# A transformer half-block's first normalisation taken inside its local attention's block

## What is computed

```
x = x + 0.5 * ffn(layernorm(x))      # first pass
x = x + attention(layernorm(x))      # 16 heads, with a line memory
x = x + 0.5 * ffn(layernorm(x))      # second pass, the same weights
```

```
h = shift_token(x)                   # the upper 64 channels come from the token before
q, k, v = split(h @ wqkv)            # 8 heads of 64
q = l2norm(q) * q_scale; k = l2norm(k) * k_scale
q, k = rotary_xpos(q, k)
o = local_attention(q, k, v)         # windows of 64: own window and the one before
x = x + o @ wo
h = layernorm(shift_token(x)) * ln_g + ln_b
a, g = split(h @ w1 + b1)
x = x + (a * gelu(g)) @ w2 + b2
```

## Time and profile before

| | us |
|---|---|
| median of three runs | 2052.03 (2050.5 to 2053.05) |
| profiled execution, its own time | 2047.57 |
| its span, first to last instruction | 2045.7 |
| PE busy | 1932.3 (94%), mean granted clock 0.974 |
| DVE busy | 1623.9 (79%) |
| ACT busy | 1502.1 (73%) |
| POOL busy | 911.3 (45%) |

### The profile page before, as it was taken

The page is one execution under the profiler, slowest core; times in us unless marked ns, Lnnn a source line. Parts: engine busy times, 40 slices in busy tenths (PEclk is TensorE's granted clock), DMA queues, the critical chain, the costliest instruction groups (busy, mean ns, idle before and its releaser), DMA issues. The chain is left out here.

```text
span 2045.7 us, 53721 instructions
## 1 busy us (share of the span) xinstructions
PE 1932.3 (94%) x19002; PEld 1163.5 (57%) x19002; DVE 1623.9 (79%) x5186; ACT 1502.1 (73%) x4129; POOL 911.3 (45%) x538
## 2 busy tenths in 40 slices
PE   6999999999999979999999978778999999999998
PEld 3677774577774334444444357426777745777753
DVE  5899974899994378999999459748999748999944
ACT  4899993699996353777777844348999946999962
POOL 1778860578870150000000046107788604888800
PEclk9999999999999986999999999899999999999999
DMA  5121220112220040111111000002122201122201
GB/s 173 42 45 43 47 65 5 34 42 46 47 67 12 0 145 30 42 43 43 43 42 41 9 3 2 1 6 46 42 47 47 65 6 33 41 47 47 63 16 42
DMA packets 75966, 84.88 MB, mean 41 GB/s; under 512 B 17124, under 2 KB 50484, under 8 KB 75572
## 3 DMA queue, kind: packets, MB, share of 16 engines
q1 hardware_dynamic: 75407, 81.41, 16.1%
q10 hardware_dynamic: 292, 0.03, 0.0%
HBM read 20.88 MB, written 8.39 MB: 14 GB/s over the span
## 5 line engine op out<-in xcount | busy, mean ns | idle before, releaser
L303 ACT ACTIVATE probs<-probs,negmax 128x128 f32<-128x128 f32 x1024 | 399.9, 396 | 25.7 <-DVE negmax L376 23.7
L1438 DVE TENSOR_REDUCE maxes<-ps_global 128x1 f32<-128x512 f32 (+3 forms) x640 | 362.2, 629 | 24.8 <-PE ps_global L1342 18.5
L1507 ACT ACTIVATE gprobs<-ps_global 128x1024 f32<-128x1024 f32 (+3 forms) x384 | 290.7, 811 | 124.1 <-PE ps_global L1379 101.8
L258 POOL TENSOR_TENSOR rot<-rot 128x1024 f32<-128x1024 f32 x128 | 302.2, 2361 | 130.1 <-DVE rot L346 130.1
L264 POOL TENSOR_TENSOR qk<-rot,cnorm 128x1024 f32<-128x1024 f32 x128 | 243.7, 1904 | 119.4 <-POOL rot L258 88.1
L271 POOL TENSOR_TENSOR probs<-probs,iden 128x1024 f32<-128x1024 f32 x128 | 242.7, 1896 | 119.1 <-DVE iden L384 119.1
L376 DVE CUSTOM_DVE_ANT_0 probs<-ps_attn,masks 128x128 f32<-128x128 f32 x1024 | 225.9, 284 | 0.0
L1337 PE MATMUL ps_global<-ks,qs 48*128 48x512 bf16 (+3 forms) x768 | 196.8, 347 | 11.4 <-DMA ks<-split_scratch 9.6
L303 ACT ACTIVATION_READ_ACCUMULATOR probs<-probs,negmax 128x1 f32 x1024 | 196.9, 192 | 0.0
L344 DVE TENSOR_TENSOR rot<-ps_attn,rotary 128x512 f32<-128x512 f32 x256 | 174.8, 683 | 11.2 <-PE ps_attn L170 8.5
L238 PEld LDWEIGHTS ps_attn<-probsT,v_first 128*64 128x64 f32 x2048 | 118.1, 136 | 98.1 <-ACT probsT L324 93.6
(11 more groups left out here) (203 smaller groups left out, 4574.7 us busy)
## 6 DMA issues: line engine op xcount, KB each, us to landing
v_first<-v_second SPq DMA_DIRECT2D x256, 128.0 KB, 2.3
hs<-z_a SPq DMA_DIRECT2D x256, 32.0 KB, 1.9
ln<-z_b SPq DMA_DIRECT2D x56, 128.0 KB, 2.3
split_scratch<-parts SPq DMA_DIRECT2D x8, 384.0 KB, 3.3
split_scratch<-gprobs SPq DMA_DIRECT2D x8, 384.0 KB, 4.7
qs<-split_scratch SPq DMA_DIRECT2D x32, 96.0 KB
ks<-split_scratch SPq DMA_DIRECT2D x32, 96.0 KB
x_tok<-in_x_dram SPq DMA_DIRECT2D x4, 512.0 KB, 6.5
```

Source lines behind the costliest of these rows:

```text
L258: nc.gpsimd.tensor_tensor(a, a, b, ALU.add).then_inc(C["rot_sum"], 1)
L303: last = nc.scalar.activation(probs[:, k % 2, slot, :], probs[:, k % 2, slot, :], ACT.Exp, scale=-1.0, bias=negmax[:, k % 2, slot:slot + 1 ...
L1438: nc.vector.reduce_max(maxes[:, n % 2, r, p0:p1, t, c], ps[:, bank_of(use), 0:len(both) * w].rearrange("q (p s) -> q p s", s=w), AX_X).the ...
L1507: nc.scalar.activation(probs[:, step % RING, 2 * p:2 * p + 2, 0:w], ps[:, S0 + 2 * p:S0 + 2 * p + 2, 0:w], ACT.Exp).then_inc(C["p2_exp"], 1)
```

## The change

The normalisation that opens a pass no longer has a block: it becomes "layer -1" of `local_attention_pass`, its six stages the functions that the layers' inner normalisations use already (`pe_centre`, `pe_var`, `act_ln_square` and so on), with three pairs of PSUM banks of its own (`FIRST_PAIRS`). The calls `body(0, -4)` to `body(0, -1)` are replaced, in both passes, by orders written out for each engine, in which chunks and the stages of tiles 0 to 3 alternate. A shift of tile 0, 4, 8 ... waits for its chunk's scale. `FirstUse`, given in the first pass only, replaces `RotaryTables` and `Folds`: `wqkv` is loaded from setup's queue, the other 14 loads behind the shifts of tiles 0 to 3; the masks' cast and seven products come ahead of scale 0 on DVE and the eighth behind it; the fold's matmuls and additions close the fill; POOL's scaling of `w1` and its cast move to the end of layer 0, ahead of `gp_ln_low`. The tables, rows and masks are loaded into the memory of `probs` and `probsT`. The normalisation ahead of the middle part stays a block.

```diff
+FIRST_PAIRS = ((3, 4), (5, 6), (7, 2))
+
+
+def local_attention_pass(nc, C, K, W, probs, probsT, z_in, z_out, x, first):
...
-            if i >= B and k % 4 == 0:
+            if k % 4 == 0 and i >= B:
                 mlp_wait1(sp, "mlp_out", 0, (BATCH_TILES * (i - B) + k) // 4)
+            elif k % 4 == 0:
+                ln_wait(sp, "ln_out", -1, (BATCH_TILES * i + k) // 4)
...
+        def ln_banks(layer, m):
+            return FIRST_PAIRS[m % 3] if layer < 0 else LN_PAIRS[m]
...
-            centred, var = LN_PAIRS[m]
-            if m == CHUNKS - 1:
+            centred, var = ln_banks(layer, m)
+            if layer < 0:
+                if m >= 3:
+                    ln_wait(pe, "ln_out", layer, m - 3)
+            elif m == CHUNKS - 1:
...
-            nc.tensor.matmul(ps[:, centred, :], K["centre"][:, :], ln_h[:, m % 4, :], start=True, stop=True
-                             ).then_inc(C["ln_centred"], 1)
+            nc.tensor.matmul(ps[:, centred, :], K["centre"][:, :], x[:, columns(m)] if layer < 0 else ln_h[:, m % 4, :],
+                             start=True, stop=True).then_inc(C["ln_centred"], 1)
...
-                if folds is not None and (i, k) == (0, -3):
-                    folds.tensor(pe, ps[:, OB, :])
...
+            pe_centre(pe, wait, -1, 0)
+            pe_centre(pe, wait, -1, 1)
+            pe_var(pe, wait, -1, 0)
+            pe_centre(pe, wait, -1, 2)
+            pe_var(pe, wait, -1, 1)
+            pe_centre(pe, wait, -1, 3)
+            pe_var(pe, wait, -1, 2)
+            pe_var(pe, wait, -1, 3)
+            pe_centre(pe, wait, -1, 4)
+            if first is not None:
+                first.tensor_projections(pe)
+            pe_project_keys(pe, wait, *t(0, 0))
+            pe_project_queries(pe, wait, *t(0, 0))
+            pe_centre(pe, wait, -1, 5)
+            pe_var(pe, wait, -1, 4)
+            pe_centre(pe, wait, -1, 6)
+            pe_var(pe, wait, -1, 5)
+            pe_project_keys(pe, wait, *t(0, 1))
+            pe_project_queries(pe, wait, *t(0, 1))
+            pe_centre(pe, wait, -1, 7)
+            pe_var(pe, wait, -1, 6)
+            pe_var(pe, wait, -1, 7)
+            pe_project_values(pe, wait, *t(0, 0))
+            wait_shifted(pe, *t(0, 2))
+            pe_project_queries(pe, wait, *t(0, 2))
+            pe_project_keys(pe, wait, *t(0, 2))
+            ln_wait(pe, "ln_out", -1, 7)
+            pe_transpose_qk(pe, wait, *t(0, 0))
+            pe_project_values(pe, wait, *t(0, 1))
+            pe_await_scores(pe, wait, *t(0, 0))
+            pe_scores(pe, *t(0, 0))
+            pe_transpose_qk(pe, wait, *t(0, 1))
+            pe_project_keys(pe, wait, *t(0, 3))
+            pe_project_queries(pe, wait, *t(0, 3))
+            pe_project_values(pe, wait, *t(0, 2))
+            pe_await_scores(pe, wait, *t(0, 1))
+            pe_scores(pe, *t(0, 1))
+            if first is not None:
+                first.tensor(pe, ps[:, OB, :])
+            pe_transpose_qk(pe, wait, *t(0, 2))
...
+                if first is not None and layer == 0:
+                    first.gpsimd(gp)
                 gp_ln_low(gp, wait, layer)
...
+            gp_rotary_sum(gp, wait, *t(0, 0))
+            gp_rotary_scale(gp, wait, *t(0, 0))
+            gp_rotary_sum(gp, wait, *t(0, 1))
+            gp_rotary_scale(gp, wait, *t(0, 1))
+            gp_rotary_sum(gp, wait, *t(0, 2))
+            gp_rotary_scale(gp, wait, *t(0, 2))
+            gp_normalise(gp, wait, *t(0, 0))
+            gp_rotary_sum(gp, wait, *t(0, 3))
...
+            act_ln_square(act, -1, 0)
+            act_ln_square(act, -1, 1)
+            act_ln_log(act, -1, 0)
+            act_ln_inverse(act, -1, 0)
+            act_ln_square(act, -1, 2)
+            act_ln_log(act, -1, 1)
+            act_ln_inverse(act, -1, 1)
+            act_ln_square(act, -1, 3)
+            act_ln_log(act, -1, 2)
+            act_ln_inverse(act, -1, 2)
+            act_ln_log(act, -1, 3)
+            act_ln_square(act, -1, 4)
+            act_ln_inverse(act, -1, 3)
+            act_square_q(act, wait, *t(0, 0))
+            act_square_k(act, wait, *t(0, 0))
+            act_ln_square(act, -1, 5)
+            act_ln_log(act, -1, 4)
+            act_ln_inverse(act, -1, 4)
+            act_ln_square(act, -1, 6)
+            act_ln_log(act, -1, 5)
+            act_norm(act, wait, *t(0, 0))
+            act_ln_inverse(act, -1, 5)
+            act_square_q(act, wait, *t(0, 1))
+            act_ln_square(act, -1, 7)
+            act_square_k(act, wait, *t(0, 1))
+            act_ln_log(act, -1, 6)
+            act_ln_log(act, -1, 7)
+            act_ln_inverse(act, -1, 6)
+            act_ln_inverse(act, -1, 7)
+            act_norm(act, wait, *t(0, 1))
+            act_values(act, wait, *t(0, 0))
+            act_square_q(act, wait, *t(0, 2))
+            act_qT(act, wait, *t(0, 0))
+            act_kT(act, wait, *t(0, 0))
+            act_square_k(act, wait, *t(0, 2))
+            act_values(act, wait, *t(0, 1))
+            act_qT(act, wait, *t(0, 1))
+            act_kT(act, wait, *t(0, 1))
+            act_norm(act, wait, *t(0, 2))
+            act_exp(act, wait, *t(0, 0), range(0, 3))
+            act_square_q(act, wait, *t(0, 3))
+            act_exp(act, wait, *t(0, 0), range(3, 8))
+            act_square_k(act, wait, *t(0, 3))
+            act_qT(act, wait, *t(0, 2))
+            act_exp(act, wait, *t(0, 1), range(0, 2))
...
+            if first is not None:
+                first.vector_tables(dve, range(0, 7))
+            dve_ln_scale(dve, -1, 0)
+            if first is not None:
+                first.vector_tables(dve, range(7, 8))
+            dve_ln_scale(dve, -1, 1)
+            dve_ln_scale(dve, -1, 2)
+            dve_rotate(dve, wait, 1, *t(0, 0))
+            dve_ln_scale(dve, -1, 3)
+            dve_rotate(dve, wait, 0, *t(0, 0))
+            dve_ssq(dve, wait, *t(0, 0))
+            dve_ln_scale(dve, -1, 4)
+            dve_rotate(dve, wait, 1, *t(0, 1))
+            dve_clip_norm(dve, wait, *t(0, 0))
+            dve_ln_scale(dve, -1, 5)
+            dve_rotate(dve, wait, 0, *t(0, 1))
+            dve_ssq(dve, wait, *t(0, 1))
+            dve_ln_scale(dve, -1, 6)
+            dve_ln_scale(dve, -1, 7)
+            dve_clip_norm(dve, wait, *t(0, 1))
+            dve_rotate(dve, wait, 1, *t(0, 2))
+            dve_rotate(dve, wait, 0, *t(0, 2))
+            dve_ssq(dve, wait, *t(0, 2))
+            dve_max(dve, wait, *t(0, 0))
+            dve_clip_norm(dve, wait, *t(0, 2))
+            dve_rotate(dve, wait, 1, *t(0, 3))
+            dve_rotate(dve, wait, 0, *t(0, 3))
+            dve_inv(dve, wait, *t(0, 0))
+            dve_max(dve, wait, *t(0, 1))
+            if first is not None:
+                first.vector(dve, ps[:, OB, :])
...
                 sp_shift(sp, wait, *t(0, tile))
+            if first is not None:
+                first.sync_loads(sp)
             sp.wait_ge(C["pass_set"], C.after("pass_set", 2))
...
+            sp.dma_start(W["wqkv"][:, :, :], dram["wqkv"].rearrange("l p n -> p l n")).then_inc(C["wqkv_in"], 16)
...
+class FirstUse:
...
     def sync_loads(self, sp):
         C, A, W, dram = self.C, self.A, self.W, self.dram
-        sp.dma_start(W["wqkv"][:, :, :], dram["wqkv"].rearrange("l p n -> p l n")).then_inc(C["wqkv_in"], 16)
-        sp.dma_start(W["wo"][:, :, :, :], dram["wo"].rearrange("l (c p) n -> p l c n", p=128)).then_inc(C["wo_in"], 16)
         sp.dma_start(W["w1"][:, :, :], dram["w1"].rearrange("l p n -> p l n")).then_inc(C["w1_in"], 16)
         for j, (f0, m) in enumerate(HID_BLOCKS):
             sp.dma_start(W["w2"][0:m, :, j, :], dram["w2"][:, f0:f0 + m, :].rearrange("l p n -> p l n")).then_inc(C["w2_in"], 16)
+        sp.dma_start(W["wo"][:, :, :, :], dram["wo"].rearrange("l (c p) n -> p l c n", p=128)).then_inc(C["wo_in"], 16)
         for name in ATTENTION_LOADS:
             dst = A[name]
             sp.dma_start(dst[tuple(slice(None) for _ in dst.shape)], dram[ATTENTION_LOADS[name]]).then_inc(C["as_in"], 16)
 
-    def tensor_last(self, pe):
+    def tensor_projections(self, pe):
         C = self.C
         pe.wait_ge(C["wqkv_in"], C.after("wqkv_in", 16))
-        pe.wait_ge(C["wo_in"], C.after("wo_in", 16))
...
+    def vector_tables(self, dve, products):
+        nc, C, K, W = self.nc, self.C, self.K, self.W
+        for m in products:
+            if m == 0:
+                dve.wait_ge(C["mask_in"], C.after("mask_in", 16))
+                nc.vector.tensor_copy(K["masks"][:, :, :], W["masks_f"])
+                dve.wait_ge(C["rotary_in"], C.after("rotary_in", 16 * N_ROWS))
+            layer, which = m // 4, m % 4
+            nc.vector.tensor_tensor(W["rotary"][:, layer, :, which, :], W["tables"][:, :, which, :],
+                                    W["rows"][:, layer, which, :].unsqueeze(1).to_broadcast([P, T // TILE, DH]), ALU.mult)
...
+        with ExitStack() as first:
+            probs, probsT = attention_probs(first)
```

(11 more changed lines are left out.)

92 lines of the change are left out of this document (23 added, 69 removed).

## The result

The changed kernel took **2017.94 us** (median of 4 runs, 2015.32 to 2019.93), the kernel before 2051.66 on the same chip; ratio **0.9835**, interval 0.9818 to 0.9852. That is 33.7 us faster, where 25.8 were forecast.

The account below looks back on a forecast made before the run. The two fills, 54.22 and 50.57 us with no engine full, were taken as what the change could shorten; gains of 13.9 and 11.9, together 25.8, off the runs' median 2052.0 gave 2026.2 us, range 2018 to 2037.

Parts of the forecast that it names:

- the yardstick: DVE's first copy of turned probabilities of tile 0: whatever brings it forward brings the layer's end forward by as much.
- the two fills: Stretches from each pass's normalisation block to DVE's first copy: 54.22 and 50.57 us, forecast to become 40.3 and 38.7.
- rival 1: Loose weave in the fills: late hops put scale 7 and the transposes 6 us later; gain 14, 2038; chance 0.20.
- Rival 2: Weave in the fills tighter than placed: 2014 to 2019 us; chance 0.05.
- Rival 3: PE stays at the lower clock level in the fills, 61 and 59 us long; slower, 2067; chance 0.04.
- Rival 4: No difference: the layer behind the fill swallows the lead; chance 0.03.
- The loads: Weight loads moved to setup's queue and behind the shifts on SP, issued until 39, would land in time.
- POOL's fold: POOL's w1 scaling and cast, 4.6 us, moved to the layer's end: fits idle time there with 2.6 to spare.
- the placement from the first keys to the copy: Fill steps placed: pass one's keys at 28.0, copy at 57.2; fills of 39.3 and 37.7 before pads.
- The pads of 1.0 for twenty hand-overs: 1.0 us added to each placed fill because the shortest hop was taken for some twenty hand-overs in a row.
- the 234 us: Time from tile 0's copy to tile 31's in each pass's first layer, 234.2 and 234.0; claimed to stay unchanged.
- The rule on ports: DVE's clips might wait up to 2.35 us beside POOL; none charged, two hits per fill would make the gain 16.

Follow-up runs that it names:

- e1: Changed kernel with pass two put back to its separate normalisation block and old body, pass one as changed: 2032.11 us, ratio 0.9912 to the kernel before.
- e2: Changed kernel with pass one put back to its separate block, products and folds, pass two as changed: 2034.11 us, ratio 0.9924 to the kernel before.
- e11: e6 with the fold's matmuls in four groups of three between steps of tiles 1 to 3: 2014.69 us, ratio 0.9828 to the kernel before.
- e4: Changed kernel with POOL's scaling of w1 and its cast moved back into the first fill: 2020.99 us, ratio 0.9854 to the kernel before.
- e5: Changed kernel without PE's wait for POOL's memsets ahead of its first matmul: 2016.08 us, ratio 0.9831 to the kernel before.
- e6: e5 with the eight rotary-table products split 4, 2 and 2 between the first scalings: 2014.86 us, ratio 0.9822 to the kernel before.
- e12: The changed kernel unaltered, run again for a second profile and time: 2017.13 us, ratio 0.9837 to the kernel before.
- e8b: Kernel before the change plus unused matmuls, three ending the normalisation block and two starting the attention block: 2045.1 us, ratio 0.9977.

## Why the prediction was right and wrong

**Right: the yardstick and the structure.** The time went where it was looked for, into the two fills, and what the fills lost the kernel gained. The first keys in pass two stand 9.3 us after the block's start (placed 9.4). The steps followed one another in the order placed: scale 7, transposes, scores, normalisation, kT of tile 2. The last scaling ends 16.8 us after the first one's start in both passes (17.6 placed), so rival 1, a loose weave, is out. Rival 2, a tighter weave, to which I gave 0.05, came in: the time lies in its 2014 to 2019. Its lower end, DVE full for the whole of pass one's fill and ACT for pass two's, was not reached (31.5 of 37.6 and 30.2 of 34.5), but from the first rotation on DVE was all but full. Rival 3 is out: the clock rose. Rival 4 is out by e1 and e2. The loads did as placed: SP's last load is issued at 38.94, the fold did not wait for its weights, and POOL's fold fits the layer's end.

**Wrong: the placement from the first keys to the copy, and the pads on it.** The fills sum to 72.03 where I had 79.0, 7.0 us less. The pads of 1.0 for twenty hand-overs, 2.0 in all, were wrong in sign. The placement itself was 1.7 too long in pass one and 3.25 in pass two. Pass two, where nothing else disturbs, tells why:

| step of pass two | placed | measured | difference |
|---|---|---|---|
| block start to first keys | 9.4 | 9.3 | -0.1 |
| first keys to transposes of tile 0 | 13.3 | 12.5 | -0.8 |
| transposes to scores | 2.7 | 1.89 | -0.8 |
| scores to first maximum | 1.9 | 2.48 | +0.6 |
| first maximum to POOL's normalisation | 6.5 | 5.20 | -1.3 |
| normalisation to DVE's copy | 3.9 | 3.08 | -0.9 |

The step that failed is the way in which I placed the work: a chain of hops from engine to engine, with DVE and ACT each left "6 us of idle time" in the fill. From DVE's first rotation to its copy this gave 27.3 us (37.7 less 9.36 and 1.06). Measured are 24.08, and DVE's own instructions fill 23.23 of them. Once tile 0 is being rotated, DVE's row of work sets the time up to the normalisation, and hops of other engines that end before DVE is ready cost nothing. The rows of pass two show it:

```profile
1351.95 0.69 DVE L345 TENSOR_TENSOR rot<-ps_attn,rotary 128x512 f32<-128x512 f32 x1 [0.21 <-PE ps_attn L171]
...
1361.47 1.21 DVE L353 TENSOR_REDUCE ssq<-sq 128x16 f32<-128x1024 f32 x1
1362.60 0.29 DVE L377 CUSTOM_DVE_ANT_0 probs<-ps_attn,masks 128x128 f32<-128x128 f32 x1
...
1363.38 0.39 ACT L304 ACTIVATE probs<-probs,negmax 128x128 f32<-128x128 f32 x1
...
1367.53 0.19 DVE L385 RECIPROCAL iden<-den 128x8 f32<-128x8 f32 x1
...
1369.75 1.09 PE L223 MATMUL ps_attn<-ident,probs 128*128 128x128 f32 x8 [0.61 <-POOL probs L272]
...
1370.88 0.69 DVE L390 COPY probsT<-ps_attn 128x512 f32<-128x512 f32 x1 [0.33 <-PE ps_attn L223]
```

Between 1351.95 and the copy DVE has no wait over 0.2 us. The maxima stand right behind DVE's sum of squares; the scores had ended at 1361.22, 1.4 us earlier, so the 0.8 that they came sooner than placed won nothing. The mis-sized terms, in the order of the path: up to the first maximum 1.1 too long, most of it from scale 5 to scale 7, for which I had 4.3 us and DVE's work is 3.6. Then 1.3 to the normalisation: I started the exponentials at 48.2, behind all eight maxima (45.9 to 47.7), and measured is the first of them 0.78 us after the start of the first maximum, so that DVE and not ACT comes last there. Last 0.9 to the copy, where eight transposes take 1.09 instead of the 1.97 of the earlier trace rows. Pass one has the same steps with 0.8, 0.8, 1.3 and 1.1 too much and 0.6 too little.

The other runs bear this out. Their profiles hold 22 fills of the changed order. In 21 of them DVE's reciprocal starts 26.1 to 26.2 us after scaling 0; in e11's first fill it is 28.1, and 1.6 of the 1.9 more lie ahead of the first keys, at a clock of 0.73 and 0.84. Behind the reciprocal they differ: 3.35 us to the copy in pass two, 3.8 to 4.1 in pass one with the fold, and 5.1 to 5.3 in e4, e5, e6 and e12, with their clock of 0.57 to 0.65. So of the 7.0 us the clock explains about 1 in each fill, by the transposes at the end, which I had taken at their old, slow length. That share is read from rows and not isolated by a run, and no run takes work off DVE ahead of the reciprocal: that it is the limit there is read from its gapless row. The projections I had placed at 0.86, their length at the full clock. e8b's 4.7 us, without any change in the order of the work, are the price that the kernel before paid for its clock, and not what the forecast missed.

**A size off the other way, hidden in pass one.** Scaling 0 was to end at 24.3 and ended at 25.8, first keys 28.0 and 29.48; from the block's start, which came 0.3 sooner, both are 1.8 late. The rows of the tables landed at 20.48 instead of 19.4, and PE's first matmuls after the boundary ran slow (3.78 us for two). I had put centring 0 at the old duration, 2.82 for three, without asking what the 2.59 us of idle time before it does to the clock, although shows just that at the old boundary. e6 removes part of it. Of the 1.8, 1.0 was left at the transposes, and the steps behind them paid it back and 1.7 more.

**The sum against runs.** The forecast set the gain against the median of the runs, 4.5 above the profiled execution. After the change the profiled execution stands 1.6 below the median, so of the 8.3 us between 2026.2 and 2017.94 only 5.4 are in the span (7.0 in the fills and 0.3 in setup, less 1.6 in the layers, and 0.3 that I do not place); 2.9 are how single executions stand to medians. How far beyond the range a set of runs falls is partly chance: 0.06 us here, 0.9 in e12. By the prediction's own chances what the range leaves out adds up to about 0.21, not "under 0.2".

**The layers.** Wrong "if the 234 us grow": they grew by 0.7 and 0.8 in this profile. Over all profiles with a changed fill they are 234.4 to 235.0 (236.3 in e4), with an old one 234.0 to 234.6. Why is open.

**The rule on ports.** The clips were charged nothing. Four of the six in the two fills stand clear of POOL's sums: their first instruction took 0.17 us, at 36.96 and 48.04 for instance. Two took 0.30 and 0.31, at 1358.10 and at 41.84, where POOL's sum (39.74, 2.37 long) ran until 42.11. The Trainium skill's SBUF — State Buffer, section "SBUF: two separate sides", agrees: the clip ended with POOL's instruction. The price was 0.14 us each, and the gain of 16 that the rule made possible did not come. The Trainium skill's TensorE: Matmul & The Clock Gate, section "What's actually happening", has idleness bring the throttled state and activity release it; e8b, whose added matmuls raised the clock, agrees.
